# Attention and a ternary feed-forward on one core: queries and keys projected as transposed chunks of 512 rows and stacked through device memory

## What is computed

```python
xn = layernorm(x)                       # 2048 rows of 256
q, k, v = xn @ Wq, xn @ Wk, xn @ Wv     # 8 query heads, 2 key/value heads of 32
q, k = rope(q), rope(k)
out = softmax(causal(q k^T / sqrt(32))) @ v
qp, kp = q[..., :3] . dir[h], k[..., :3] . dir[h]      # one number per row and head
geo_out = softmax(causal(qp[t] * kp[s])) @ v
out = out + head_scales * (geo_out - out)
attn = out @ Wo
z = xn @ ternary(W_syn).T + b_syn       # 1024 columns, ternary weights
hidden = where(z >= the row's 102nd largest, relu(z), 0)
ffn = layernorm(xn + hidden @ ternary(W_out).T + b_out) * gamma + beta
result = x + attn + ffn
```

## Time and profile before

| | us |
|---|---|
| runs of the kernel | 772.93, 773.45, 773.46 (median 773.45) |
| the profiled execution | 772.55, of which span 770.6 |
| TensorE busy in the span | 699.5 (91%) |
| DVE, ACT, POOL busy | 499.1, 464.7, 262.5 |
| mean granted TensorE clock | 0.936 of 2.4 GHz |

### The profile page before, as it was taken

One profiled execution on the slowest core, in us unless ns is written; L12 is line 12 of the kernel. 1 busy time (PEld: TensorE's weight loads), 2 busy tenths in 40 slices (PEclk: granted clock), 3 DMA queues, 4 the chain that ended last, 5 costly groups with the idle time before them and its releaser, 6 DMA issues. The chain is left out here.

```text
span 770.6 us, 12758 instructions
## 1 busy us (share of the span) xinstructions
PE 699.5 (91%) x4536; PEld 327.3 (42%) x4536; DVE 499.1 (65%) x1022; ACT 464.7 (60%) x789; POOL 262.5 (34%) x390
## 2 busy tenths in 40 slices
PE   2766789999999999999999999999899999988993
PEld 1443335333434444443444445444445455553532
DVE  3798478764386886377777873655776666667602
ACT  3352655335753544875443547888889889868650
POOL 5514453332431312331101203324424533356532
PEclk9885889698999999999999999899999999999996
DMA  8100000000000000000000000000000000000000
GB/s 240 61 1 4 6 1 8 1 1 3 1 8 1 1 1 1 3 1 1 6 3 1 1 1 10 1 1 8 16 7 9 8 8 15 8 8 2 1 1 27
DMA packets 12372, 9.40 MB, mean 12 GB/s; under 512 B 5713, under 2 KB 11729, under 8 KB 12306
## 3 DMA queue, kind: packets, MB, share of 16 engines
q1 hardware_dynamic: 12306, 8.55, 3.8%
HBM read 5.80 MB, written 2.10 MB: 10 GB/s over the span
## 5 line engine op out<-in xcount | busy, mean ns | idle before, releaser
L731 ACT ACTIVATE probs<-scores 128x1024 f32<-128x1024 f32 (+3 forms) x320 | 270.0, 893 | 202.9 <-PE acc L1216 188.3
L929 DVE TENSOR_REDUCE piece_max<-side 128x1 f32<-128x512 f32 x192 | 127.9, 686 | 54.5 <-PE side L1110 53.3
L1209 PE MATMUL acc<-probs,v_nat 128*32 128x512 f32 (+3 forms) x1280 | 157.1, 564 | 5.3 <-POOL probs L608 3.9
L1216 PE MATMUL acc<-probs,ones_all 128*32 128x512 f32 (+3 forms) x1280 | 155.4, 558 | 0.0
L608 POOL TENSOR_SCALAR_AFFINE_SELECT probs<-probs 128x256 f32<-128x256 f32 x128 | 56.3, 451 | 184.1 <-ACT probs L731 182.7
L1110 PE MATMUL side<-k_stack,q_stack 96*128 96x512 f32 (+3 forms) x290 | 112.6, 442 | 3.9 <-DVE piece_max L929 3.6
L1191 PE MATMUL scores<-q_stack,k_stack 98*128 98x512 f32 (+3 forms) x320 | 90.2, 384 | 5.6 <-ACT probs L731 5.3
L1110 PEld LDWEIGHTS side<-k_stack,q_stack 96*128 96x128 f32 x290 | 51.4, 194 | 96.2 <-DVE piece_max L929 45.2
L955 DVE RECIPROCAL d_raw<-d_raw 128x512 f32<-128x512 f32 x16 | 53.6, 3347 | 34.7 <-ACT o_raw L744 34.7
L1191 PEld LDWEIGHTS scores<-q_stack,k_stack 98*128 98x128 f32 x320 | 53.0, 190 | 36.0 <-ACT probs L731 27.1
L1195 PE MATMUL scores<-q_geo,k_geo 10*128 10x512 f32 (+3 forms) x320 | 58.0, 468 | 6.6 <-ACT probs L731 6.3
(11 more groups left out here) (143 smaller groups left out, 1024.5 us busy)
## 6 DMA issues: line engine op xcount, KB each, us to landing
res<-in_L_attn_x_dram SPq DMA_DIRECT2D x4, 512.0 KB, 9.2
out_dram<-res SPq DMA_DIRECT2D x16, 128.0 KB, 1.7
z_buf<-in_L_ffn_W_syn_dram SPq DMA_DIRECT2D x1, 1024.0 KB, 7.7
z_buf<-in_L_ffn_W_out_dram SPq DMA_DIRECT2D x1, 1024.0 KB, 4.8
k_geo<-geo_rows SPq DMA_DIRECT2D x24, 8.0 KB
q_geo<-geo_rows SPq DMA_DIRECT2D x24, 8.0 KB
w_qkv<-in_L_attn_Wq_dram SPq DMA_DIRECT2D x1, 256.0 KB, 4.2
tables<-in_cos_table_dram SPq DMA_DIRECT2D x1, 256.0 KB, 4.5
```

The lines of the kernel that those rows point to most:

```text
L731: nc.scalar.activation(probs[:, slot % 2, pair, :, off:], scores[:, pair, :, off:], ACT.Exp, scale=ATT_SCALE if kind == 0 else 1.0).then_i ...
L929: free(nc.vector.tensor_reduce(piece_max[:, h, p:p + 1], pt, AX.X, ALU.max), ("S",) + a)
L1209: nc.tensor.matmul(acc[D * h:D * h + D, 0, off:], v_nat[:, j, g], probs[:, slot_no[a] % 2, h // 2, h % 2, off:], start=(j == 0), stop=(j = ...
L1216: last = nc.tensor.matmul(acc[D * h:D * h + D, 1, off:], ones[:, 0:D], probs[:, slot_no[a] % 2, h // 2, h % 2, off:], start=(j == 0), stop ...
```

## The change

Four things change.

1. **Projection.** The normalised rows of a chunk are transposed in two units of four transposes into `xnT` of 512 columns. The weights are then stationary and 512 rows move: three units `qA`, `qB`, `qK` of two matmuls each give the first halves of all query heads, the second halves, and the keys, already transposed. The values come from a unit `v` of eight matmuls of 64 columns. The rotary tables are needed transposed too: they are spread over heads (ACT for chunk 0, POOL for the others), turned by 48 transposes on TensorE (`tT`) and, for chunks 1 to 3, parked in device memory. The weights are sorted once on DVE (`w_sort`). The geometric numbers come from two matmuls (`gx`) with small direction matrices.
2. **Stacking.** High and low parts of queries and keys are written to device memory, and read back head by head into the three blocks of 32 rows of `q_stack` and `k_stack`: per chunk four writes and six reads on SP.
3. **Parking.** `xn` holds only one chunk. The chunk and its transpose are written to device memory; the feed-forward reads a tile of the transpose (`xz`) in place of the second transposes, and a tile of the rows (`xb`).
4. **The planner.** New prices, a table of `TURN` prices by pair of modes that count before the start is chosen, other ranks, landing times and a new rule for when a bank may be taken. Constants move: the fills of `k_geo` and `q_geo` go from POOL to DVE, the products of `geo_max` too, the loads of weights and tables from SP to ACT's queue.

```diff
-TURN = 110
+TURN = {("full", "columns"): 235, ("rows", "columns"): 215, ("columns", "full"): 145, ("columns", "rows"): 145,
+        ("full", "rows"): 220, ("rows", "full"): 220}
...
-            unit("qkv", 2 * c, ("xT", t), 220, [("xn", t)])
-            unit("qkv", 2 * c, ("qkv", t), 1300, [("xnT", t)] + ...)
-                unit("heads", 2 * c, ("qT", t, half), 440, [("split", t), ("q_twin", t)])
-            unit("heads", 2 * c, ("kT", t), 440, [("split", t), ("geo_dots", t)])
+        for s in "ABK":
+            unit("proj", 2 * c, ("q" + s, c), 1790, [("xnT", c, 0), ("xnT", c, 1)] + [("w_sort",)] * (c == 0))
+        unit("proj", 2 * c, ("v", c), 1250, [("xnT", c, 0), ("xnT", c, 1)])
+        unit("gx", 0, ("gx", c), 1780, [("join", c, "A"), ("join", c, "K")] + [("dirs",)] * (c == 0))
...
-            start = max(ready, clock[eng])
+            start = max(ready, clock[eng] + (TURN.get((mode, m), 0) if eng == "pe" else 0))
...
+                if k in ("stack_hi", "stack_lo"):
+                    sp.wait_ge(lo_out if part else hi_out, 32 * (c + 1))
+                    for r in ((1,), (0, 2))[1 - part]:
+                        sp.dma_start(k_stack[D * r:D * r + D, :, cols].bitcast(F32),
+                                     k_parked[c, part].rearrange("(d g) t -> d g t", g=G)).then_inc(stack_in[c], 16)
+                    for r in ((2,), (0, 1))[1 - part]:
+                        sp.dma_start(q_stack[D * r:D * r + D, b].bitcast(F32),
+                                     q_parked[c, part].rearrange("(d h) t -> d h t", h=H)).then_inc(stack_in[c], 16)
...
                     if a[0] == "S":
-                        if h % HG == 0 and p == 0:
-                            consumed(pe, ("kT", t))
-                            consumed(pe, ("qT", t, h // HG))
+                        if col == 0 and h == 0 and p == 0:
+                            pe.wait_ge(stack_in[c], 16 * 6)
```

More of the change, by code:

```diff
@@ L35 @@
 GROWS = 5
+KROWS = G * D
+COLS = 3 * P + KROWS
+ANG = 3 * HALF
 BANKS = 2
@@ L57, in unit @@
         add(flow, "pe", rank, ("unit",) + name, ns, after, "full")
+    turned = []
+    for c in range(NCH):
+        for s in range(3):
+            rank = 0 if c == 0 else 0.5
+            add("spread", "act" if c == 0 else "pool", rank, ("spread", c, s), 650 if c == 0 else 1300, [("tables",)] + turned[-2:-1])
+            unit("trig", rank, ("tT", c, s), 450, [("spread", c, s)])
+            add("trig", "act", rank, ("t_put", c, s), 600, [("unit", "tT", c, s)] + [("t_park", c - 1)] * (c > 1), empties=("tT", c, s))
+            turned.append(("unit", "tT", c, s))
+        if c:
+            add("t_park", "sp", 0, ("t_park", c), 550, [("t_put", c, s) for s in range(3)])
+    add("w_sort", "dve", 0, ("w_sort",), 2000, [("w",)])
+    add("dirs", "dve", 0.5, ("dirs",), 500, [("dir_in",)])
     for c in range(NCH):
@@ new lines, in build_plan @@
+            add("norm", "act", 1, ("xn", t), 400, [("shift", c)] + [("unit", "xT", c - 1, 1), ("xn_park", c - 1)] * (c > 0))
+        add("park", "sp", 2, ("xn_park", c), 550, [("xn", t) for t in tiles])
+        for i in range(2):
+            unit("xT", 2 * c, ("xT", c, i), 480, [("xn", TPC * c + 2 * i), ("xn", TPC * c + 2 * i + 1)])
+            add("xnT", "act", 0, ("xnT", c, i), 600, [("unit", "xT", c, i)]
+                + [("unit", "v", c - 1), ("unit", "qK", c - 1), ("unit", "qB", c - 1), ("xnT_park", c - 1)] * (c > 0), empties=("xT", c, i))
@@ new lines, in build_plan @@
+        add("geo_in", "act", 0, ("geo_in", c), 1200, [("unit", "gx", c)]
+            + [("geo_hi", c - 1), ("geo_top", c - 1), ("geo_lo", c - 1)] * (c > 0), empties=("gx", c))
+        add("split", "act", 1, ("khi", c), 600, [("join", c, "K")])
+        add("split", "act", 1, ("hi", c), 1130, [("join", c, "A"), ("join", c, "B")])
+        add("split", "dve", 0 if c == 0 else ROPE_RANK, ("klo", c), 620, [("khi", c), ("unit", "gx", c)])
+        add("split", "dve", 0 if c == 0 else ROPE_RANK, ("lo", c), 1170, [("hi", c), ("unit", "gx", c)])
@@ L180, in build_plan, with held_up @@
             emptied_by.setdefault(o[4], []).append(key)
-    gates = {}
-    for name, keys in emptied_by.items():
-        own, seen = ("unit",) + name, list(keys)
-        for r in seen:
-            seen += [d for d in op[r][2] if d in op and own in op[d][2] and d not in seen]
-        gates[own] = tuple(d for r in seen for d in op[r][2] if d != own and d not in seen)
+    ahead = {}
+    for keys in queue.values():
+        ahead.update(zip(keys[1:], keys))
+    def held_up(key, own):
+        if key in done or key not in op or key == own:
+            return False
+        if op[key][0] == "pe":
+            return True
+        return any(held_up(d, own) for d in op[key][2] + ((ahead[key],) if key in ahead else ()))
     bank = {}
@@ L225, in build_plan @@
                     after = after + (other,)
-            if any(d not in done for d in gates.get(key, ())):
+            if key[0] == "unit" and any(held_up(r, key) for r in emptied_by[key[1:]]):
                 continue
@@ new lines, in _ @@
+                if k == "geo_rows":
+                    c, side_ = key[1:]
+                    sp.wait_ge(geo_lo_ready, c + 1)
+                    if side_ == 0:
+                        geo_key_rows(sp, c)
+                    else:
+                        if c >= 1:
+                            sp.wait_ge(probs_used, acc_done[epi_no[(c - 1, G - 1, 1)]])
+                        if c == 0:
+                            sp.wait_ge(geo_filled, 2)
+                        for g in range(G):
+                            hs_ = slice(HG * g, HG * g + HG)
+                            for r, src in enumerate((geo_hi[hs_, 1], geo_hi[hs_, 1], geo_lo[hs_, 1])):
+                                at = GROWS * g + r
+                                sp.dma_start(q_geo[at:at + 97:32, g, :].bitcast(F32), src.bitcast(F32)).then_inc(geo_in[c], 16)
```

574 lines of the change are left out of this document (357 added, 217 removed).

## The result

| | us |
|---|---|
| the kernel before, 8 runs | 773.19 (770.77 to 773.75) |
| the change, 8 runs | 777.17 (775.72 to 782.52) |
| ratio | 1.0067, 95% interval 1.0045 to 1.0088 |
| the profiled execution of the change | 776.62, span 774.9 |

A forecast was written before the change was run, and what follows sets the result against it. TensorE was taken as the bound, busy 699.5 of 770.6 us and nearly always from 86.4 us on. Savings of 8 + 13 + 16 = 37 us from 772.55 gave 736 us, range 712 to 762.

The forecast's parts named there:

- Term 1: TensorE's projection, transposes and geometric numbers: less work at full clock, 8 us less (6 to 10).
- Term 2: TensorE's mode changes, 609 before and 482 after: 127 x 0.10 gives 13 us less, ends nothing and 20.
- Term 3: The start: first geometric score at 53 us in place of 86.4; 16 us less net, ends 3 and 30.
- The stated signs: First geometric score between 47 and 60 us, wrong if after 65; first standard score of chunk 1 near 200.
- The four us for exposed chains: Taken off the start's 20 us saved: part of a chunk's chain of parkings, table and stack shows on TensorE.
- more than 50 us of attention: Chunks 2 and 3: attention listed between each parking DMA and its reader covers the DMA, so it costs nothing.
- Of the DMAs nothing: Parking DMAs, some 26 MB over the whole span at 34 KB per us, were costed at nothing.
- Half-rate stacks: Stack reads into 32 rows run at half rate, S of chunk 0 begins 9 us later: 745 us; chance 0.08.
- Slower, by SP's queue: Feed-forward tiles stuck behind waits on SP's queue run after attention: 781 us; chance 0.07.
- No change: Same TensorE time, only the order moved, early start eaten by chunk 1's chain: 773 us; chance 0.03.

The follow-up runs named there:

- Run 1: The kernel before with the change's TURN table, start rule, bank rule and prices, its data path as it was: 776.14 us, ratio 1.0045.
- run 7: The change with every entry of its TURN table set to 200 ns, 347 mode changes in place of 482: 797.98 us, ratio 1.0337.
- run 13: The kernel before with the planner's price of a mode change 60 in place of 110: 799.4 us.
- run 16: The change with the planner's SLACK 110 in place of 120, 498 mode changes in place of 482: 797.8 us.

## Why the prediction was wrong

**Term 1, TensorE's work: right.** 8 less was forecast; the priced work went from 573 to 564, 9 less. Projection and geometric numbers at full clock, against the 1.85 and 1.85 that the term had:

```profile
320.14 1.98 PE L1291 MATMUL side<-xnT,w_qkv 128*128 128x512 f32 x4
321.96 1.89 PE L1295 MATMUL side<-w_qkv,xnT 128*128 128x64 f32 x16
323.67 0.48 PE L1349 MATMUL side<-up_T,xs_hi 128*128 128x512 f32 x1
...
326.19 1.05 PE L1303 MATMUL side<-turned,dirs_q 24*40 24x512 f32 x2
327.08 1.02 PE L1304 MATMUL side<-turned,dirs_k 6*40 6x512 f32 x2
328.03 0.51 PE L1399 MATMUL scores<-q_geo,k_geo 10*128 10x512 f32 x4
```

1.82 and 1.84; the sixteen records of the values take 1.71 per chunk, 6.8 in all where 5.6 was chosen between 3.7 and 7.7.

**Term 2, "127 x 0.10 gives 13 us less": the step that failed in size.** The price of one change was read rightly in one place, and does not sum up. In the split above the rest is 87.7 us before (609 changes) and 86.0 in the change (482): 2 us where 13 were forecast. Run 1 has 2 as well (85.5). The lower end of the term, nothing, had been argued from ACT's exp. Beside it, the order that groups by mode is another order, with other waits, and the loss to the clock went from 38.5 to 44.4 us. From 135 further changes removed (run 7) the rest did fall by 15, so the price is not nothing; why the first 127 gave so little stays open.

**Term 3, "53 us in place of 86.4" and "16 us less": failed at its first link.** The chain was begun at the shift on DVE, put at 13 us, 2 later than before; it came out at 22. In DVE's list the sorting of the weights stands ahead of it, and the last of the weights, which ACT's queue issues behind the two tables, landed just before 20.4:

```profile
20.38 0.71 DVE L1032 COPY w_qkv<-probs 128x256 f32<-128x256 f32 x2 [12.31 <-DMA probs<-in_L_attn_Wv_dram]
...
21.99 0.15 DVE L1026 SCALAR_TENSOR_TENSOR shift<-mean_var,rstd 128x4 f32<-128x4 f32 x1
```

TensorE's first transpose, of an angle table, waited for the sine table on the same queue (ACT could spread it at 18.0). The prediction named the wait for the weights, had the row that warned (a table's issue of 2.43 us) and charged 2 us for it, and even the lower end of the term had the shift at 18; the issue behind the tables took 6.6. With one table the shift stands at 12 and the first geometric score at 54, where it was put: 53 was the time of the kernel with that fault mended. Within the rest of the chain two errors partly cancel. From the shift to the end of `geo_top` 34.5 us were priced and 31.7 measured; from there to the score 5.5 were priced and 11.4 measured, since the four issues of the maxima stand behind stack reads on SP's queue and land 5.3 us after the last of them, where 1.7 was taken:

```profile
53.03 0.68 DVE L1119 TENSOR_TENSOR maxima<-maxima 8x512 fp32r<-8x512 f32 x1
57.37 2.38 SPq L660 DMA_DIRECT2D q_geo<-maxima  x4
65.08 0.80 PE L1399 MATMUL scores<-q_geo,k_geo 10*128 10x512 f32 x4 [0.38 <-DMA q_geo<-maxima]
```

The stated signs said as much: 65.1 is over the 65 named as a sign of being wrong, and the first standard score of chunk 1 came at 224 where 200 was expected.

**The four us for exposed chains: failed.** From the first geometric score of chunk 0 to that of chunk 1 the kernel before loses 18 us of TensorE's time and the change 31 (other orders of the old data path 18 to 20, of the new one 26 to 34). No single wait holds it: the waits there are below 1.5 us each. Of the split, the loss to the clock holds the most, 13.5 against 4.7. Most of that is where the count begins. Both kernels run at the lower clock from about 50 to 76 us:

```profile
50.00:77.00 27.00, 15.86 (x45) 8.38 (x44) 22.87 (x52) 6.52 (x13) 9.58 (x9) 0.51 0.01 3
51.00:75.00 24.00, 15.33 (x67) 8.04 (x68) 9.15 (x16) 13.05 (x22) 3.36 (x7) 0.51 0.68 189
```

Before (first line) all of it lies ahead of the first geometric score; in the change (second line) ten us of it lie behind. Counted from the start to the first geometric score of chunk 1, the clock takes 16 us before and 19 in the change. The stack of chunk 3, which "more than 50 us of attention" was to cover, was waited for 5.1 us: the preparation of chunk 3 sits close ahead of its `S` in the list, not far.

**"Of the DMAs nothing": failed in part.** The bytes were counted (35.5 MB in place of 9.4), but by their mean over the span. They come in bursts, at a DMA share of 0.99 between 330 and 340, and TensorE stands at the end of one for 5.1 us.

**The rivals.** None of them gave the number. *Half-rate stacks* had its place right, the `S` behind a stack, and its rate wrong: 13 us for the 1.9 MB is 149 KB per us, two thirds of the 218 taken, with 0.6 MB of other transfers in the same time, and alone the shape costs a third more, not twice. *Slower, by SP's queue* is not what happened in the change, whose last product of the feed-forward ends at 735 and whose attention at 755, though its 781 is as near to the measured time as any, by chance; but its mechanism, feed-forward left over at the end, is run 13, at 26 us, in the kernel before. *No change* at 773, "only the order moved; if the early start is eaten by chunk 1's chain", is as near, on the other side, and had 0.03; the early start was eaten indeed, at chunk 1 and in chunk 2.

**What no term had: the order.** The sum compared two kernels as if the rest of their time stayed as it was. All 1100 or so entries of TensorE's list were reordered, and orders of the same work lie between 765 and 798. The old settings give a favourable order for the kernel before (others of its orders: 776, 777, 799), and the change's settings give an ordinary one for the new data path (others: 765, and 779 to 798). A range of 712 to 762 could not hold that; some 15 us on either side had to be in it. How much of the missing gain is luck of this kind cannot be said closely: the mean over four pairs of settings is 6 us less for the new data path with the planner rules that come with it, with a spread from 19 less to 2 more.

What stays open is what lowers the clock where TensorE hardly waits, as from 290 to 297 in the change, and whether any rule of the planner would find the favourable orders; only their times were compared.

## What to carry to other kernels

When a change alters a planner's inputs, time two or three neighbouring settings of both kernels before giving the difference a cause: here one such number moved the time by up to 26 us, and the change's own effect was 4. Read the first instruction of the new critical chain down to the DMA that feeds it; a table read in short runs cost 11 us, and packing it in one was the steadiest gain of the study. A wait on a busy TensorE can cost much more than its length through the clock behind it (15.3 us for one of 4.0 in run 16) or little more (6.9 for one of 5.1 in the change), so look at the granted clock right after each wait of several us, and test by taking the wait away before the low clock is put down to it.

## What the hardware showed that was not expected

- Behind a wait of 4.0 us the granted clock stood at its lower level for 34 us, with TensorE busy 32.7 of them; behind one of 5.1 us in another order, for 7, and with that wait taken away a low stretch of 7 us came six us later all the same.
- Two angle tables in runs of 64 and 128 bytes, 384 KB together, took 16.7 us for the second to land and held ACT's queue 6.6 us at the next issue; the same bytes in runs of 3 KB landed in 4.2 us and the next issue took 0.54. The Trainium skill, DMA: Bandwidth & Descriptors, Specifications, puts the least run for full rate at 512 bytes; by that the trace agrees.
- 512 KB into 32 rows took 4.7 us and into 128 rows 3.5; three such at once 9.7 and 7.3, one measurement each.
